# Four fused layers over 16 batches: the Fori loop written out, the running sum by one triangle and pair sums, and a new step order

## The reference, cut to what matters

```python
# x: (16, 256, 256) float32; each stage keeps that shape
x = layernorm(x + attn0(x))      # steps a_...  spectral mixing
x = layernorm(x + ffn0(x))       # steps g_...  gated low-rank experts
x = layernorm(x + attn1(x))      # steps b_..., e_...  16-head softmax attention
x = layernorm(x + ffn1(x))       # steps c_...  ternary weights, 256 -> 1024 -> 256

def attn0(x):
    qf  = normalise(fft(x @ W_q.T))       # per head of 16 values
    kvf = normalise(fft(x @ W_kv.T))
    kvf = cumsum(kvf, axis=1)             # the running sum over the 256 rows
    return ifft(qf * kvf).real @ W_o.T
```

## Time and profile before

| what | value |
|---|---|
| median of 3 runs | 925.77 us (925.53 to 926.23) |
| span of the profiled execution | 926.8 us |
| PE busy | 758.7 us (82%) |
| DVE busy | 659.5 us (71%) |
| POOL busy | 535.1 us (58%) |
| ACT busy | 508.8 us (55%) |
| mean granted TensorE clock | 0.921 of full speed |

### The profile page before, as it was taken

One profiled execution on the slowest core, in us unless ns is written; L12 is line 12 of the kernel. 1 busy time (PEld: TensorE's weight loads), 2 busy tenths in 40 slices (PEclk: granted clock), 3 DMA queues, 4 the chain that ended last, 5 costly groups with the idle time before them and its releaser, 6 DMA issues.

```text
span 926.8 us, 17535 instructions
## 1 busy us (share of the span) xinstructions
PE 758.7 (82%) x5932; PEld 593.6 (64%) x5932; DVE 659.5 (71%) x1631; ACT 508.8 (55%) x929; POOL 535.1 (58%) x442
## 2 busy tenths in 40 slices
PE   4162777888989889989898989898999997987762
PEld 3141555576868677868686867777777776765452
DVE  3846475878888877888688878887888888757120
ACT  0030342748484848494748475756666665673520
POOL 3605050518585856585667667775858583545654
PEclk9585887999999998999999999999999999999866
DMA  6100404040404030303022220303040403030000
GB/s 188 45 12 0 80 1 81 1 81 2 81 13 70 24 70 23 69 23 69 24 52 39 53 40 35 57 35 58 7 85 8 74 14 68 36 47 1 12 12 11
DMA packets 112044, 39.40 MB, mean 43 GB/s; under 512 B 102440, under 2 KB 105456, under 8 KB 111984
## 3 DMA queue, kind: packets, MB, share of 16 engines
q1 hardware_dynamic: 111984, 38.71, 20.3%
HBM read 21.66 MB, written 16.78 MB: 41 GB/s over the span
## 4 chain that ended last, share of the span: by engine, by line
PE 49%; DVE 22%; ACT 14%; issue 8%; POOL 5%; DMA 1%; DVEq 0%; POOLq 0%; SPq 0%; ACTq 0%
PE pA L481 8%; ACT kT L815 6%; PE pB L586 5%; PE pC L669 5%; PE pS L608 4%; ACT qT L815 4%; PE pA L499 4%; PE pC L689 4%; PE pA L511 3%; PE pS L646 3%; PE pO L624 3%; DVE nmax L1205 3%; PE pA L467 3%; PE pB L575 2%; ACT pt L826 2%
## 5 line engine op out<-in xcount | busy, mean ns | idle before, releaser
L1339 POOL TENSOR_TENSOR rn<-ss,minus_half 128x16 f32<-128x16 f32 x64 | 188.5, 2958 | 64.4 <-DVE ss L1017 64.4
L826 ACT ACTIVATE pt<-pS 128x512 f32<-128x512 f32 x256 | 149.5, 612 | 97.0 <-PE pS L608 95.6
L1205 DVE TENSOR_REDUCE nmax<-pB 128x2 f32<-128x512 f32 x256 | 166.3, 684 | 32.1 <-PE pB L586 31.5
L1390 POOL TENSOR_TENSOR hid_lo<-hr,hid 128x512 fp32r<-128x512 f32 x64 | 91.0, 1422 | 20.8 <-ACT hid L866 20.8
L608 PE MATMUL pS<-qT,kT 98*128 98x256 bf16 x512 | 96.2, 283 | 1.6 <-DMA qT<-nmaxT 1.0
L586 PE MATMUL pB<-kT,qT 96*128 96x256 bf16 x512 | 89.5, 276 | 6.9 <-ACT kT L815 3.9
L1366 POOL TENSOR_TENSOR hr<-hr 128x512 f32<-128x512 f32 x64 | 68.2, 1066 | 37.4 <-ACT hr L847 37.4
L1371 POOL TENSOR_TENSOR hsum<-hsum,hsq 128x512 f32<-128x512 f32 x48 | 61.2, 1275 | 48.7 <-ACT hsq L859 48.7
L669 PE MATMUL pC<-x3T,w1T 128*128 128x256 f32 x256 | 73.7, 317 | 8.3 <-DVE x3T_lo L1264 4.9
L624 PE MATMUL pO<-pt,v_ext 128*32 128x256 f32 x1024 | 68.9, 387 | 3.9 <-ACT pt L826 3.9
L689 PE MATMUL pC<-w2T,hid 128*128 128x256 f32 x256 | 68.2, 303 | 1.4 <-DVE ms L1268 1.4
(11 more groups left out here) (182 smaller groups left out, 1942.9 us busy)
## 6 DMA issues: line engine op xcount, KB each, us to landing
qkv_scratch<-qkv SPq DMA_DIRECT2D x16, 768.0 KB, 3.2
pos<-qkv_scratch SPq DMA_DIRECT2D x16, 768.0 KB, 7.0
xa<-in_x SPq DMA_DIRECT2D x16, 256.0 KB, 2.7
out_y<-y SPq DMA_DIRECT2D x16, 256.0 KB, 2.0
pt<-in_wfc SPq DMA_DIRECT2D x1, 1024.0 KB, 6.4
pt<-in_wproj SPq DMA_DIRECT2D x1, 1024.0 KB, 4.8
qkv<-in_const SPq DMA_DIRECT2D x1, 512.0 KB, 3.8
x<-in_qkvT SPq DMA_DIRECT2D x2, 256.0 KB
```

What stands on the lines that cost most here:

```text
L826: act.activation(pt[:, (h // 4) % 2, h % 4].rearrange("p s n -> p (s n)"), pS[h % 2][:], ACT.Exp).then_inc(S["probs"], 1)
L1205: dve.tensor_reduce(nmax[:, h * SIDES:(h + 1) * SIDES], pB[h % 2][:].rearrange("p (s k) -> p s k", s=SIDES), AX.X, ALU.max, negate=True).t ...
L1339: pool.tensor_tensor(rn[:].rearrange("p s m -> p (s m)")[:, at], ss[:].rearrange("p s m -> p (s m)")[:, at], minus_half[:, at], ALU.pow).t ...
L1390: pool.tensor_tensor(hid_lo[:, 2 * g:2 * g + 2].rearrange("p c n -> p (c n)"), hr[:, g % 2, :], hid[:, 2 * g:2 * g + 2].rearrange("p c n - ...
```

## The change

- `turns` writes out every turn; there is no loop. A step name may carry a shift, as in `b_rows:+1` or `e_score_0:-1`, which adds to its lag: the step is emitted one turn later (at the head of the next turn) or earlier (at its end) for the same batch. One more turn is emitted for the shifted steps.
- `a_pair`, new on POOL, adds the two sides of the key spectrum (128x256) into `pair`, which lies in `raw_spec`. `a_cum` multiplies `upto` once with `pair`; the result is the sum up to and with the odd row. `a_cum0`, new on DVE, subtracts side 1 from it for the even row, from PSUM into PSUM. The triangle `below` leaves the constants.
- All five lists have a new order.

SP's list becomes `b_rows:+1 c_store:+1 g_write g_read p_load`. Seen from one turn: `g_write`, `g_read`, `p_load`, and then, ahead of the next `g_write`, `b_rows` and `c_store`. At the join PE's list runs `... e_wo a_attn c_ms b_maxt_t c_y e_score_0 | a_xt g_x1t ...`.

```diff
             def a_cum(i, k):
-                pe.wait_ge(S["spectra"], nth(i, PER["spectra"], 2))
-                for s in range(SIDES):
-                    for r in range(SIDES):
-                        mask = masks["upto" if r <= s else "below"]
-                        ins = pe.matmul(pA[0][:, s * D:(s + 1) * D], mask, spec[:, r, :, 1, :],
-                                        start=(r == 0), stop=(r == SIDES - 1))
-                ins.then_inc(S["cum_ready"], 1)
+                pe.wait_ge(S["pair_sum"], nth(i, PER["pair_sum"], 1))
+                pe.matmul(pA[0][:, D:2 * D], upto, pair, start=True, stop=True).then_inc(S["cum_ready"], 1)
...
+            def a_cum0(i, k):
+                dve.wait_ge(S["cum_ready"], nth(i, PER["cum_ready"], 1))
+                dve.wait_ge(S["spectra"], nth(i, PER["spectra"], 2))
+                dve.tensor_tensor(pA[0][:, 0:D].rearrange("p (c n) -> p c n", c=2),
+                                  pA[0][:, D:2 * D].rearrange("p (c n) -> p c n", c=2), spec[:, 1, :, 1, :],
+                                  ALU.subtract).then_inc(S["cum0"], 1)
...
             def a_cross(i, k):
-                dve.wait_ge(S["cum_ready"], nth(i, PER["cum_ready"], 1))
-                dve.wait_ge(S["spectra"], nth(i, PER["spectra"], 2))
+                dve.wait_ge(S["cum0"], nth(i, PER["cum0"], 1))
...
+            def a_pair(i, k):
+                pool.wait_ge(S["spectra"], nth(i, PER["spectra"], 2))
+                if has(i):
+                    pool.wait_ge(S["cum_ready"], before(i, PER["cum_ready"]))
+                pool.tensor_tensor(pair, spec[:, 0, :, 1, :], spec[:, 1, :, 1, :], ALU.add
+                                   ).then_inc(S["pair_sum"], 1)
...
-            with eng.Fori(0, (BATCHES - lead) // 2) as j:
-                turn(j * 2 + lead, lead % 2)
-                turn(j * 2 + (lead + 1), (lead + 1) % 2)
+            for t in range(BATCHES + max(LAG.values()) + 1):
+                if t in ahead:
+                    ahead[t]()
+                turn(t)
```

The middle and the end of PE's list, before and after:

```diff
-    ... e_score_14 c_hid_3 e_score_15 b_max_7 b_max_8 a_cum e_out_3 b_max_9 b_max_10 g_qkv_1
-    e_outt_0 b_max_11 e_outt_1 b_max_12 g_qkv_2 b_max_13 e_ont b_max_14 a_prt b_max_15 e_wo b_maxt_t
-    c_ms a_attn c_y
+    ... e_score_14 b_max_7 g_qkv_0 b_max_8 a_cum e_score_15 b_max_9 c_hid_3 e_out_3 b_max_10 g_qkv_1
+    e_outt_0 b_max_11 b_max_12 e_outt_1 g_qkv_2 b_max_13 e_ont a_prt b_max_14 b_max_15 e_wo a_attn
+    c_ms b_maxt_t c_y e_score_0:-1
...
-    p_load g_write b_rows g_read c_store
+    b_rows:+1 c_store:+1 g_write g_read p_load
```

More of the change, by code:

```diff
@@ L58, in shape_constants @@
     upto = np.triu(np.ones((P, P)))
-    below = np.triu(np.ones((P, P)), 1)
     n = np.arange(HD)[:, None]
@@ L74, in shape_constants @@
     inv /= HD
-    out = [ident, upto, below, np.tile(np.arange(EXPERTS, 0, -1.0), (P, 1))]
+    out = [ident, upto, np.tile(np.arange(EXPERTS, 0, -1.0), (P, 1))]
     for m in (fwd, inv):
@@ L82, in shape_constants @@
     return np.concatenate(out, axis=1).astype(np.float32)
-CONST_COLS = 3 * P + EXPERTS
+CONST_COLS = 2 * P + EXPERTS
 DFT_COLS = 2 * CH * D
@@ L93 @@
 ORDER = (
[6 rows of a table removed]
-    "c_ms a_attn c_y "
[12 rows of a table removed]
[L116 to L122, removed]
[5 rows of a table added]
+    "e_outt_1 g_qkv_2 b_max_13 e_ont a_prt b_max_14 b_max_15 e_wo a_attn c_ms b_maxt_t c_y e_score_0:-1 "
[13 rows of a table added]
+    "e_mean a_bn a_mean e_norm "
+    "a_pow1 c_pow c_norm c_h_0:-1 c_lo_0:-1 a_root_0:-1 a_root_1:-1 g_pow2:-1 a_root_2:-1 c_h_1:-1 "
+    "a_root_3:-1 c_add_1:-1 a_pair:-1 c_lo_1:-1 c_h_2:-1 c_add_2:-1 c_lo_2:-1 c_h_3:-1 c_add_3:-1 "
+    "c_lo_3:-1 c_hsum:-1 c_rms:-1 e_pow:-1 "
+    "b_rows:+1 c_store:+1 g_write g_read p_load "
 ).split()
@@ L127 @@
     x_in=16, qkv_out=16, pos_in=16, max_in=32, y_out=16,
-    xt_ready=1, proj_ready=2, proj_sb=2, cum_ready=1, prt_ready=1, attn_ready=1, x1t_ready=1, gate_ready=1,
+    xt_ready=1, proj_ready=2, proj_sb=2, pair_sum=1, cum_ready=1, cum0=1, prt_ready=1, attn_ready=1, x1t_ready=1, gate_ready=1,
     mixt_ready=1, ffn_ready=1, x2t_ready=1, qkv_ready=3,
@@ L156, in mega_kernel @@
         ident = cst[:, 0:P]
-        masks = {"upto": cst[:, P:2 * P], "below": cst[:, 2 * P:3 * P]}
+        upto = cst[:, P:2 * P]
         desc = cst[:, CONST_COLS - EXPERTS:CONST_COLS]
@@ L262, in mega_kernel @@
         prodT = raw_spec[:, 1, :]
+        pair = raw_spec[:, 0, 0:D].rearrange("p (c n) -> p c n", c=2)
         onT = oS[:, 0:2, :].rearrange("p g n -> p (g n)")
@@ L303, in turns, with turn @@
         def turns(eng, steps, ahead=()):
[L306 to L309, removed]
+            def turn(t):
+                for entry in ORDER:
+                    name, _, shift = entry.partition(":")
+                    lag = LAG[name[0]] + int(shift or 0)
+                    if not 0 <= t - lag < BATCHES:
                         continue
                     if name in steps:
-                        if isinstance(t, int) and (t, name) in ahead:
+                        if (t, name) in ahead:
                             ahead[t, name]()
[L314 to L318, removed]
+                        steps[name](t - lag, (t - lag) % 2)
+            for t in range(BATCHES + max(LAG.values()) + 1):
                 if t in ahead:
                     ahead[t]()
-                turn(t, t % 2)
-            with eng.Fori(0, (BATCHES - lead) // 2) as j:
-                turn(j * 2 + lead, lead % 2)
-                turn(j * 2 + (lead + 1), (lead + 1) % 2)
-            for t in range(BATCHES, BATCHES + last):
-                turn(t, t % 2)
+                turn(t)
         block = ctx.enter_context(nc.Block())
@@ L1027, in _, with a_cross @@
             cross = raw_spec[:, 0, :].rearrange("p (s c n) -> p s c n", s=SIDES, c=2)
-            def a_cross(i, k):
+            def a_cum0(i, k):
                 dve.wait_ge(S["cum_ready"], nth(i, PER["cum_ready"], 1))
                 dve.wait_ge(S["spectra"], nth(i, PER["spectra"], 2))
+                dve.tensor_tensor(pA[0][:, 0:D].rearrange("p (c n) -> p c n", c=2),
+                                  pA[0][:, D:2 * D].rearrange("p (c n) -> p c n", c=2), spec[:, 1, :, 1, :],
+                                  ALU.subtract).then_inc(S["cum0"], 1)
+            def a_cross(i, k):
+                dve.wait_ge(S["cum0"], nth(i, PER["cum0"], 1))
                 cum = pA[0][:].rearrange("p (s c n) -> p s c n", s=SIDES, c=2)
@@ L1286, in c_mean @@
                 mean(mvc, stc, S["c_var"])
-            steps = dict(a_xt_lo=a_xt_lo, a_sums=a_sums, a_cross=a_cross, a_res1=a_res1, a_bn=a_bn, a_mean=a_mean,
+            steps = dict(a_xt_lo=a_xt_lo, a_sums=a_sums, a_cum0=a_cum0, a_cross=a_cross, a_res1=a_res1, a_bn=a_bn, a_mean=a_mean,
                          a_norm1=a_norm1, g_res2=g_res2, g_bn=g_bn, g_mean=g_mean, g_norm2=g_norm2,
@@ L1399, in c_pow @@
                 root(rsc, vec_, S["c_pow"])
-            steps = dict(a_pow1=a_pow1, g_pow2=g_pow2, e_pow=e_pow, c_hsum=c_hsum, c_rms=c_rms, c_pow=c_pow, c_norm=c_norm)
+            steps = dict(a_pair=a_pair, a_pow1=a_pow1, g_pow2=g_pow2, e_pow=e_pow, c_hsum=c_hsum, c_rms=c_rms, c_pow=c_pow, c_norm=c_norm)
             for n in range(4):
```

## The result

The changed kernel takes 1000.4 us (median of 4 runs, 998.75 to 1001.06), the kernel before 925.65 beside it: ratio 1.081, 95% interval 1.077 to 1.084. I had forecast 964 with a range of 940 to 984. The direction and the largest term, a wait for late transfers at each turn's end, are as forecast; the loss is twice as large, 75 us in place of 38, because other terms of the sum were wrong.

The account below looks back on a forecast made before the run. PE, busy 82% of the span, was the main bound, with waits and stretches of DVE work in the chain. On 926.8 us, -13.2 - 15.4 + 57.4 + 4 + 5.6 = +38.4 gave 965.2, as median 964; range 940 to 984.

Parts of the forecast that it names:

- Jumps: At the loop's 4 jumps back: writing the loop out removes 3 x 3.0 + 4.2 us, a credit of -13.2 us.
- The new wait: At turn ends PE stalls at `e_score_0` for late load and rows: 14 x 4.1 = 57.4 us, plus 4 us at turns 16, 17.
- I price them alike: Ends of early turns, without `c_y` to cover the stall, were priced at the same 4.1 us as later ones.
- The clock: Behind each stall PE runs slower: 0.4 us a turn, 5.6 us; priced by the whole stretch's loss, 1.7 a turn, 24.
- The rest of the order: Other moves on DVE, POOL and the other lists: priced 0, with 0.4 us a turn either way, 6 us.
- the delay of `a_norm1`: DVE and POOL moves delay `a_norm1` and `g_x1t` up to 1 us; free behind the stall, otherwise 0 to 14 us.
- The pair sum: From `a_cum` to `e_ont`: fewer PE products gain 0.9 to 1.3 us a turn, taken as 1.1 over 14 turns, -15.4 us.
- rival (c): At `a_cum`: it waits for POOL, or the saved 1.3 us ends in another wait behind `a_cross`; 979 us, chance 0.15.
- (a): At turn ends: load and rows land by 438.0, so the transfers are hidden and the kernel is faster; 904 us, chance 0.1.
- (b): At turn ends: small transfers overtake, the stall is 3.1 instead of 4.1 us with little clock loss; 949 us, chance 0.15.

## Why the prediction was right and wrong

The account in full turns, from PE's timelines: the mark is `b_maxt_t`, turn 3 the first with one, and the mean is over the 11 distances from turn 5 to turn 16, whatever lies between.

| kernel | mark of turn 5, us | mean turn, us | span, us |
|---|---|---|---|
| before | 240.2 | 47.66 | 926.8 |
| loop out | 239.9 | 46.09 | 909.5 |
| + new order, SP's list old | 232.9 | 48.56 | 930.5 |
| + pair sum (change with SP's old list) | 227.5 | 47.21 | 908.7 |
| + SP's new list, fillers in the hole | 249.5 | 50.75 | 981.8 |
| the change | 249.3 | 52.75 | 999.0 |

In medians, as a sum beside that of the prediction: loop -13.6 (forecast -13.2), order +18.6 (0), pair sum -20.3 (-15.4), holes +70.2 (+61.4), clock +19.9 (+5.6). Together +74.8 against +38.4; the terms of order and pair sum hold for this sequence of steps only. So of the 36 us missed the clock makes 14, order and pair sum together 14 (+13.7), and the holes 9. These kernels were not all timed together; by their ratios to the kernel before, order and pair sum come to 17 and 20.

- **Jumps: right.** Written out alone they give 12.4 us beside the kernel before timed with it, 13.6 by the medians above. The profiled executions are 17.3 apart: the turns behind a jump went from 49.3 to 45.9, but those without one from 46.3 to 45.9 too, which was not foreseen. The 4.2 of the first jump held a longer stretch at the low clock (0.52 from 346 to 353 us, against 0.75 in the earlier trace rows).
- **The new wait: right in kind and place, and in a full turn in size.** The load behind the read of turn 2 in the earlier trace rows was the right model: its issue takes 4.21 us (4.13 there), landing 7.5, PE held at `e_score_0` for 4.03 to 4.38 us at the ends of turns 6 to 15 but one (5.24, behind an issue of 5.60). Too small were the others. "I price them alike" failed: the end of turn 2 cost 6.3, those of turns 3 to 5 9.15, 9.15 and 5.07; in turns 3 and 4 no `c_y` stands ahead to cover any of it, and at the end of turn 5 the load's issue took 5.67. The last two cost 3.45 and 4.79 where I took 2. All holes together are 80.5 us; the kernel with fillers, which keeps their length, is 70 above the one without them.
- **The clock: the first step that failed.** I took 0.4 us a turn, from how much longer a turn with a 2.73 us hole was than the hole itself, and set aside 1.7 a turn, the price by the granted clock of the earlier trace rows. Measured: 22.0 us in the 11 turns between the change and the kernel with fillers, 2.0 a turn. My 0.4 was a small difference between whole turns and a hole, and carried whatever else moved in those turns; the earlier trace rows showed the loss itself, 1.7 us behind a hole of 2.73, and a hole of 4.2 lost about 2. The prediction even had the range 0.3 to 1.4, whose upper end is the first jump with its long stretch at the low clock; in the change five of eleven turns have a long one too. The Trainium skill, "TensorE: Matmul & The Clock Gate", section "Why this matters for your kernels", lists a DMA wait in each round of a loop as the bad case; the runs agree. The 24 us that I worked out from the earlier trace rows lie nearer to the 20 measured than my 5.6.
- **The rest of the order: the second step that failed.** "The other moves cross no wait that I can price; 0, with 0.4 us a turn either way", and the delay of `a_norm1` hidden by the stall: without that stall the order costs 18.6 us, 2.5 in a full turn, partly given back by a head of the kernel that is 7 us shorter at turn 5. From `b_max_0` to `a_cum` PE takes 9.27 us in place of 8.55, though `c_hid_3` and `e_score_15` were moved out of this stretch. It now contains a wait of 0.95 us for the row maxima that DVE reads behind `a_spectra_1`, stretched to 1.77 us beside `c_add_1`; with that overlap gone, the stretch fell from 9.28 to 8.20 in the changed kernel with SP's old list. From `a_cum` to `e_outt`, where the two steps went, it is 5.82 in place of 4.66, and from `a_proj_0` to `b_stack` 0.5 to 1.2 us more. What each other move causes was not separated. With the stall in place this last part is gone (7.67 us, and 7.62 in the old order), as the prediction had it for the delay of `a_norm1`; whether that delay is what is hidden is not shown. Its 0.85 us a turn count in the order's term above and are missing from that of the holes.
- **The pair sum: right in its 1.3 us, wrong as a sum.** I asked only which chain ends at `e_ont` and bounded the gain from below by 0.9; with the old order DVE ended the whole stretch and there was no gain, with the new one it was 20. With the order it came in, the two together make -1.7 us in place of -15.4. That is near rival (c)'s size, "the saved 1.3 us ends in another wait", but not its mechanism of POOL: PE waits for `a_pair` once, 19.1 us in turn 1, where before it waited for the spectra, and not in the full turns.
- **The rivals.** (a), hidden transfers at 904, is out for this order; its 904 is near the kernel with SP's old list (910), which has no such transfers to hide. (b), small transfers that overtake: the rows were seen landing behind the load, at 521.39 against 521.03 (513.53 + 7.5), and the hole was 4.2, not 3.1. The Trainium skill, "DMA: Bandwidth & Descriptors", section "Queues, rings and completion order", lets completions come in another order. No row here shows it: the rows landed 0.36 us behind the load, 2.90 us after their issue in place of 1.9, and those 1.0 us are what separates 4.2 from 3.1.

Open: why the new order with the pair sum reaches `b_maxt_t` of turn 3 some 10 us sooner when SP's list is the old one (137.97 against 147.70 with the loop out), and which of its moves, beside the one that put `a_spectra_1` next to `c_add_1`, cost 2.5 us a turn.

## What to carry to other kernels

Before a transfer is put behind another on the same issuing engine, look in the trace for one place where that sequence already occurs: here a single pair of rows in turn 2 (4.13 us) gave the blocked issue to 0.2 us in 11 of 14 turns (4.15 to 4.29; the others 4.85 to 5.67), and the block fell on SP's next issue, whether that was the load or the rows. A recurring hole on PE costs its length and then the slower clock of the work behind it; price the second part from the granted clock and the stretched instructions of a window behind such a hole, not from differences between whole turns. A saving on one engine is worth what the next engine in the stretch lets through, so ask, for each reordering, which engine ends last with the saving made.

## What the runs showed of the hardware

- The issue of a 256 KB load, 0.55 us behind that of a 768 KB read in 64-byte pieces, takes 4.2 us on SP; the first of two 8 KB issues in its place, 1.06 us behind the read, takes 3.75. Both end 4.8 us after the start of the read's issue. It is the position behind the read that costs, not the size of what follows; whether it is the read's size or its small pieces was not varied.
- Sixteen needless matmuls (3.8 us of PE a turn) in front of a wait made the kernel 20 us shorter: from `a_xt` to `a_proj_0` it is 2.76 us with them and 3.9 to 5.1 without.
- The low clock also follows shorter waits, and not each time: behind the same wait of 1.75 us the granted clock was 0.75 over 6.81 us in one turn and 1.00 in another of the same execution, a difference of 1.2 us.
- A 128x512 product on DVE takes 0.69 us alone, 0.68 beside a 2.90 us `a_root` of 128x16 on POOL, and 1.77 beside a 128x512 addition on POOL; a 128x512 bf16 copy on DVE took 0.28 us in one kernel and 1.36 in another, there beside a 1.73 us instruction of POOL. In the trace of before, 1.09 us for the same product beside such an addition was already a stretched one: POOL ended at 418.44, 0.69 more is 419.13, DVE ended at 418.98.
